# Layer 1's routed experts on gathered rows in plain f32, with the shared expert behind the last head

## The reference

```python
aff = jax.nn.sigmoid(flat_x @ gate_w + expert_bias)
_, topk_idx = jax.lax.top_k(aff, TOP_K)                    # TOP_K = 2
mask = (topk_idx[:, :, None] == jnp.arange(E_r)[None, None, :]).any(axis=1)
_, sel_idx = jax.lax.top_k(jnp.where(mask, aff, -1.0).T, capacity)   # 1024 // 7 = 146
kept = jnp.take_along_axis(mask.T, sel_idx, axis=1)
w = jnp.where(kept, jnp.take_along_axis(aff.T, sel_idx, axis=1), 0.0)
out = jax.vmap(_ffn)(flat_x[sel_idx], routed_w1, routed_w2)   # x1 * silu(x2) @ w2, F = 128
routed_sum = jnp.zeros_like(flat_x).at[sel_idx].add(out * w[:, :, None])
x = x + attention + (shared_sum + routed_sum)
```

## Time and profile before

| | |
|---|---|
| median of 3 runs | 812.11 us (811.54 to 812.62) |
| the profiled execution | 811.76 us, span 809.8 us |
| PE busy | 726.8 us, 4180 matmuls |
| DVE, ACT, POOL busy | 549.9, 370.9, 337.7 us |
| layer-1 experts, about | 557 to 637 us |

### The profile page before, as it was taken

One profiled execution on the slowest core, in us unless ns is written; L12 is line 12 of the kernel. 1 busy time (PEld: TensorE's weight loads), 2 busy tenths in 40 slices (PEclk: granted clock), 3 DMA queues, 4 the chain that ended last, 5 costly groups with the idle time before them and its releaser, 6 DMA issues.

```text
span 809.8 us, 12520 instructions
## 1 busy us (share of the span) xinstructions
PE 726.8 (90%) x4180; PEld 572.4 (71%) x4180; DVE 549.9 (68%) x1099; ACT 370.9 (46%) x783; POOL 337.7 (42%) x250
## 2 busy tenths in 40 slices
PE   3899999999889999999999999998999899765467
PEld 1455666678568888888888999987889446554356
DVE  4256566540679889897979667673667744499995
ACT  2264111110356474747474747555554531576541
POOL 0000375600167565656566666552111110337661
PEclk9999999999899999999999999999999999978798
DMA  9400000000310101010101000001110000100001
GB/s 311 186 1 2 1 1 1 1 1 1 103 46 21 33 19 32 19 32 19 32 19 32 20 32 19 19 7 40 40 39 0 1 0 1 33 1 0 0 1 52
DMA packets 11327, 24.75 MB, mean 31 GB/s; under 512 B 1217, under 2 KB 5538, under 8 KB 10786
## 3 DMA queue, kind: packets, MB, share of 16 engines
q1 hardware_dynamic: 10928, 23.19, 8.7%
q10 hardware_dynamic: 370, 1.18, 0.5%
HBM read 23.31 MB, written 1.05 MB: 30 GB/s over the span
## 4 chain that ended last, share of the span: by engine, by line
PE 66%; DVE 21%; issue 7%; ACT 3%; DMA 2%; POOL 1%; DVEq 1%; SPq 0%; POOLq 0%; ACTq 0%
PE bank L474 11%; PE bank L493 8%; PE bank L495 8%; PE bank L494 8%; PE bank L483 7%; PE bank L661 4%; PE bank L570 3%; PE bank L691 2%; PE bank L690 2%; DVE x L1439 2%; PE bank L675 2%; DVE zone L1616 2%; PE bank L537 2%; DVE arena L1423 1%; DVE arena L1413 1%
## 5 line engine op out<-in xcount | busy, mean ns | idle before, releaser
L493 PE MATMUL bank<-zone 128*128 128x256 f32 (+1 forms) x520 | 180.5, 347 | 9.5 <-DVE arena L1414 4.3
L495 PE MATMUL bank<-zone 128*128 128x256 f32 (+1 forms) x520 | 170.0, 327 | 0.0
L494 PE MATMUL bank<-zone 128*128 128x256 f32 (+1 forms) x520 | 169.8, 327 | 0.0
L493 PEld LDWEIGHTS bank<-zone 128*128 128x128 f32 x520 | 99.5, 191 | 26.1 <-DVE arena L1414 9.8
L1750 POOL TENSOR_TENSOR arena<-arena 128x512 f32<-128x512 f32 x64 | 82.0, 1282 | 84.3 <-ACT arena L1048 75.5
L495 PEld LDWEIGHTS bank<-zone 128*128 128x128 f32 x520 | 99.5, 191 | 8.8
L494 PEld LDWEIGHTS bank<-zone 128*128 128x128 f32 x520 | 99.7, 192 | 6.6
L1755 POOL TENSOR_TENSOR arena<-arena 128x512 f32<-128x512 f32 x64 | 82.4, 1287 | 32.3 <-DVE arena L1414 23.1
L1744 POOL TENSOR_TENSOR zone<-arena,zone 128x512 fp32r<-128x512 f32 (+1 forms) x56 | 58.4, 1056 | 60.8 <-ACT zone L1110 47.9
L474 PE MATMUL bank<-xT,arena 128*128 128x512 f32 x160 | 78.1, 626 | 1.5 <-ACT xT L937 0.8
L1067 ACT ACTIVATE arena<-arena 128x256 f32<-128x256 f32 (+1 forms) x128 | 62.1, 487 | 32.8 <-DVE arena L1423 32.7
(11 more groups left out here) (266 smaller groups left out, 1460.6 us busy)
## 6 DMA issues: line engine op xcount, KB each, us to landing
arena<-in_qk SPq DMA_DIRECT2D x16, 256.0 KB, 2.7
arena<-in_tern SPq DMA_DIRECT2D x1, 3072.0 KB, 21.9
arena<-in_wv SPq DMA_DIRECT2D x8, 256.0 KB, 2.7
arena<-in_wo SPq DMA_DIRECT2D x16, 128.0 KB, 2.1
arena<-in_w SPq DMA_DIRECT2D x8, 256.0 KB, 2.8
lB<-in_lB SPq DMA_DIRECT2D x1, 1288.5 KB, 24.3
arena<-in_lA SPq DMA_DIRECT2D x1, 1282.5 KB, 15.2
x<-in_x SPq DMA_DIRECT2D x1, 1024.0 KB, 12.8
```

Source lines behind the costliest of these rows:

```text
L493: pe.matmul(dst, lhi, rhi, start=(n == 0), stop=False)
L494: pe.matmul(dst, lhi, rlo, start=False, stop=False)
L495: last = pe.matmul(dst, llo, rhi, start=False, stop=(n == len(terms) - 1 and not open_end))
```

## The change

- The choice: `weigh_tokens` also scans, per expert, the number of each chosen token and adds 146 times the expert (C_OFF), which gives each (token, expert) a slot of 1022, or 0.
- Routes: after head 10 PE turns weights and slots (`turn_routes`, 16 transposes), waits for DVE's copies (`wcol_ready`), and DVE makes from them for each token two row indices (`idx`) and two weights (`wtok`) (`find_rows`).
- Scatters: POOL sends the normalised rows, 16 indirect DMAs of 128 rows, into `xg_rows` in DRAM, in heads 11, 12 and 13. A token without a slot is skipped by the bounds check. SP loads the rows back, by slot, as `xg`.
- Between heads 13 and 14: PE transposes `xg`, and runs the seven routed experts on 146 columns each, in plain f32. Each result is stored by SP in `y_rows`, as 80 and 66 rows. Row 1022 is zero.
- POOL then gathers for each token its two rows (16 indirect DMAs), before, between and behind the turnings of head 14; DVE adds them by weight: the first ones in head 15, the second ones before the shared expert's result is added.
- The shared expert, still split, comes after head 15. The Fori loops of the heads stop earlier, and heads 10 to 15 are partly straight code. The head's queue orders are otherwise as before.
- SP's loads: all routed weights at once, 3584 columns at the start of the layer and 1792 behind the gathered rows, in place of a pair of experts at a time.
- The arenas move: xT now also holds `xg`, and xn1 the second gather; qraw has room of its own.

```diff
+        xg_rows = nc.dram_tensor("xg_rows", (T, D), F32, kind="Internal").ap()
+        y_rows = nc.dram_tensor("y_rows", (SLOTS + 1, D), F32, kind="Internal").ap()
...
+            sp.wait_ge(kvbd_ready, 1)
+            sp.dma_start(xg_rows.rearrange("(t p) d -> p t d", p=P), kvbd[:, 0:1, :].to_broadcast([P, NT, D])).then_inc(rows_cleared, 16)
+            sp.dma_start(y_rows[SLOTS:SLOTS + 1, :], kvbd[0:1, 0, :]).then_inc(rows_cleared, 16)
...
+            sp.dma_start(wr[0], dram["wr"][:, 0:EXP_A]).then_inc(wr_loaded, 16)
+            with sp.Fori(0, SPLIT // 2) as i:
+                next_wv(i)
...
+                    next_wqk(i * 2 + c)
+                    next_wo(i * 2 + c)
+            next_wqk(SPLIT)
+            sp.wait_ge(scattered, 2 * NT * 16)
+            sp.dma_start(xg, xg_rows.rearrange("(t p) d -> p t d", p=P)).then_inc(xg_loaded, 16)
+            sp.dma_start(wr[1], dram["wr"][:, EXP_A:]).then_inc(wr_loaded, 16)
+            sp.wait_ge(wv_split, H1 // 2)
+            sp.dma_start(w1s, dram["w1s"]).then_inc(w1s_loaded, 16)
+            sp.wait_ge(wqk_split, H1)
+            sp.dma_start(w2s, dram["w2s"]).then_inc(w2s_loaded, 16)
+            for e in range(ER):
+                sp.wait_ge(*g_r2[e].ready)
+                sp.dma_start(y_rows[e * CAP:e * CAP + LEAD, :], yg[0:LEAD, e, 0:D]).then_inc(y_stored, 16)
+                sp.dma_start(y_rows[e * CAP + LEAD:(e + 1) * CAP, :], yg[2 * LEAD - CAP:LEAD, e, D:2 * D]).then_inc(y_stored, 16)
+            next_wo(SPLIT)
...
+            def turn_routes():
+                pe.wait_ge(wsel_ready, 1)
+                pe.wait_ge(rope_half, 4 * (ROUNDS // 2 + 2) + 3)
+                for n, table in enumerate((wT1, sT)):
+                    for t in range(NT):
+                        at = (n * NT + t) * ER
+                        last = pe.transpose(ps[0][:, at:at + ER], table[:, tok(t)], ident[0:ER, 0:ER])
+                last.then_inc(bank_full[0], 1)
+            def routed_in(e):
+                g = g_r1[e]
+                reuse(g)
+                for n in range(2):
+                    for k in range(KD):
+                        last = pe.matmul(g.ps[:, n * CAP:(n + 1) * CAP], expert(e, k * D + n * P, P), xgT[:, k, e * CAP:(e + 1) * CAP],
+                                         start=(k == 0), stop=(k == KD - 1))
+                last.then_inc(g.full_sem, 1)
+            def routed_out(e):
+                g = g_r2[e]
+                reuse(g)
+                pe.wait_ge(rhid_ready, e + 1)
+                for n, at in enumerate((0, CAP - LEAD)):
+                    last = pe.matmul(g.ps[0:LEAD, n * D:(n + 1) * D], rhid[e % 3][:, at:at + LEAD], expert(e, KD * D, D), start=True, stop=True)
+                last.then_inc(g.full_sem, 1)
...
+            with pe.Fori(0, SPLIT // 2 - 2) as i:
-            head(H1 // 2 - 1, 0)
-            head(H1 // 2 - 1, 1, False, False)
+            head(SPLIT // 2 - 2, 0)
+            turn_routes()
-            with pe.Fori(0, E1 // 2) as i:
+            head(SPLIT // 2 - 2, 1)
+            head(SPLIT // 2 - 1, 0)
+            head(SPLIT // 2 - 1, 1)
+            pe.wait_ge(xg_loaded, 16)
+            for b in range(NB):
+                for k in range(KD):
+                    g = g_tx[b][k]
+                    reuse(g)
+                    for tt in range(TPB):
+                        last = pe.transpose(g.ps[:, tok(tt)], xg[:, b * TPB + tt, tok(k)], ident)
+                    last.then_inc(g.full_sem, 1)
+            pe.wait_ge(wr_loaded, 16)
+            for e in range(ER):
+                if e == 0:
+                    pe.wait_ge(xg_act, KD)
+                if e == BW // CAP:
+                    pe.wait_ge(xg_dve, KD)
+                if e == EXP_A // EXP_W:
+                    pe.wait_ge(wr_loaded, 32)
+                routed_in(e)
+                if e >= 2:
+                    routed_out(e - 2)
+            routed_out(ER - 2)
+            routed_out(ER - 1)
+            for left in HEAD1["left"]:
+                pe.wait_ge(*left)
+            head(H1 // 2 - 1, 0, True, True, HEAD1)
+            head(H1 // 2 - 1, 1, False, False, HEAD1)
+            shared_in()
+            shared_out()
...
+            def routed_silu(e):
+                g = g_r1[e]
+                act.wait_ge(*g.full)
+                if e >= 3:
+                    act.wait_ge(*g_r2[e - 3].full)
+                act.activation(rhid[e % 3], g.ps[:, CAP:2 * CAP], ACT.Silu).then_inc(rsilu_ready, 1)
+            def keep_y(e):
+                g = g_r2[e]
+                act.wait_ge(*g.full)
+                act.activation(yg[0:LEAD, e, :], g.ps[0:LEAD, :], ACT.Copy).then_inc(g.ready_sem, 1)
+            for e in range(ER):
+                routed_silu(e)
+                if e >= 2 and e % 2 == 0:
+                    keep_y(e - 2)
+            keep_y(ER - 1)
+            act.wait_ge(w1s_loaded, 16)
+            act.activation(w1s2[0].bitcast(F32R), w1s, ACT.Copy).then_inc(w1s_hi, 1)
+            act.wait_ge(w2s_loaded, 16)
+            act.activation(w2s2[0].bitcast(F32R), w2s, ACT.Copy).then_inc(w2s_hi, 1)
...
+            dve.wait_ge(rows_cleared, 32)
...
+                chain(dve.scalar_tensor_tensor(out=wT1, in0=sT[:, 0:T], scalar=TAKEN, in1=sT0, op0=ALU.is_equal, op1=ALU.mult))
+                chain(dve.tensor_scalar(sT0, wT1, 0.0, None, ALU.is_gt))
+                chain(dve.tensor_tensor_scan(affT, sT0, sT0, 0.0, ALU.add, ALU.max))
+                dve.scalar_tensor_tensor(out=sT[:, 0:T], in0=affT, scalar=const[0:ER, C_OFF:C_OFF + 1], in1=sT0,
+                                         op0=ALU.add, op1=ALU.mult).then_inc(wsel_ready, 1)
+            def find_rows():
+                dve.wait_ge(bank_full[0], TURNED)
+                step(dve.tensor_copy(kwt, ps[0][:, 0:NT * ER].rearrange("p (t e) -> p t e", t=NT)), dve_done)
+                k = step(dve.tensor_copy(ktab, ps[0][:, NT * ER:2 * NT * ER].rearrange("p (t e) -> p t e", t=NT)), dve_done)
+                after(k)
+                dve.sem_inc(wcol_ready, 1)
+                chain(dve.tensor_reduce(dest[:, 0, :], ktab, AX.X, ALU.max))
+                chain(dve.tensor_reduce(dest[:, 1, :], ktab, AX.X, ALU.add))
+                chain(dve.tensor_tensor(dest[:, 1, :], dest[:, 1, :], dest[:, 0, :], ALU.subtract))
+                chain(dve.tensor_tensor(kown, ktab, dest[:, 0, :].unsqueeze(2).to_broadcast([P, NT, ER]), ALU.is_equal))
+                chain(dve.tensor_tensor(kown, kwt, kown, ALU.mult))
+                chain(dve.tensor_tensor(kwt, kwt, kown, ALU.subtract))
+                step(dve.tensor_reduce(wtok[:, 0, :], kown, AX.X, ALU.add), dve_done)
+                step(dve.tensor_reduce(wtok[:, 1, :], kwt, AX.X, ALU.add), dve_done)
+                chain(dve.tensor_scalar(miss, dest, 0.0, float(SLOTS + 1), ALU.is_equal, ALU.mult))
+                chain(dve.scalar_tensor_tensor(out=dest, in0=dest, scalar=-1.0, in1=miss, op0=ALU.add, op1=ALU.add))
+                dve.tensor_copy(idx.rearrange("p (s t) -> p s t", s=2), dest).then_inc(idx_ready, 1)
+            def add_rows(s, t):
+                dve.wait_ge(gathered[(s * NT + t) // TPB], TPB * 16)
+                dve.scalar_tensor_tensor(out=x[:, t, :], in0=got[s][:, t, :], scalar=wtok[:, s, t:t + 1], in1=x[:, t, :],
+                                         op0=ALU.mult, op1=ALU.add).then_inc(combined, 1)
...
+                if last:
+                    x_is(4 * h + base["added"])
+                    for t in range(NT):
+                        add_rows(0, t)
...
+            def routed_product(e):
+                g = g_r1[e]
+                dve.wait_ge(*g.full)
+                dve.wait_ge(rsilu_ready, e + 1)
+                dve.tensor_tensor(rhid[e % 3], g.ps[:, 0:CAP], rhid[e % 3], ALU.mult).then_inc(g.ready_sem, 1)
+            for e in range(ER):
+                routed_product(e)
...
+            x_is(4 * H1 + HEAD1["added"])
+            for t in range(NT):
+                add_rows(1, t)
+            for p in range(NT // 2):
+                dve.wait_ge(combined, NT + 2 * p + 2)
+                x_is(g_s2[p].ready[1] - 1)
+                add_pair(g_s2[p], p)
+                x_is(g_s2[p].ready[1])
+                measure((2 * p, 2 * p + 1))
+                if p % 2:
+                    normalise(2, xn2, p // 2)
...
+            def send_rows(ns):
+                for n in ns:
+                    pool.indirect_dma_start(xg_rows, bass.IndirectOffsetOnAxis(idx[:, n:n + 1], 0), xn1[:, n % NT, :], None,
+                                            bounds_check=SLOTS - 1, oob_is_err=False).then_inc(scattered, 16)
+            def fetch_rows(ns):
+                for n in ns:
+                    pool.indirect_dma_start(got[n // NT][:, n % NT, :], None, y_rows, bass.IndirectOffsetOnAxis(idx[:, n:n + 1], 0),
+                                            bounds_check=SLOTS, oob_is_err=False).then_inc(gathered[n // TPB], 16)
+            def beside_head(h, base=HEAD0, between=lambda: None):
```

(23 more changed lines are left out.)

342 lines of the change are left out of this document (170 added, 172 removed).

## The result

The changed kernel takes **791.29 us** (median of 4 runs, 790.22 to 795.84), the kernel before beside it on the same chip 811.92: a ratio of 0.9758, 95% interval 0.9732 to 0.9785. It is faster by 2.4%, 20.6 us. The forecast was 780 with 767 to 797: right in sign, 11 us too hopeful. The profiled execution of after took 792.32 against 811.76, a gain of 19.4; it is the one that I take apart.

A forecast was written before the change was run, and what follows sets the result against it. PE, busy 90% of 809.8 us, was taken to bound the kernel. The sum was 811.8 - 58.5 + 1 + 3 + 14 + 1.8 + 7.2 = 780.3, so 780 us, range 767 to 797.

The forecast's parts named there:

- Removed, 58.5: Last head's output product (end S) to layer 2's second transpose block: 25 us in place of 83.5, so 58.5 saved.
- (a), (b): Tables in head 9, 1 us reaching PE; turning the routes after head 10, 3 us with a lower clock.
- (c): Routed experts between heads 13 and 14: 14 us added, 6.6 for seven experts' products, 3 for clock and late load.
- (d): Row DMAs in POOL's queue ahead of weights PE wants: 1.8 us in head 12, 7.2 in heads 14 and 15.
- E: Time one row DMA holds POOL: taken as 1.1 us, with 0.33 and 2.6 kept as bounds.
- free up to E = 1.6: Head 11: five scatters on POOL cost PE nothing unless each holds POOL longer than 1.6 us.
- Rival 1: Gathers cheap, each holding POOL 0.65 us or less: heads 14 and 15 lose nothing, 772 or 768 us; chance 20%.
- rival 3: POOL held for each row DMA's whole transfer: stalls in heads 11 to 15, slower, 819 us at 2.6 each; chance 4%.
- my own case: Each row DMA holds POOL between 0.7 and 1.4 us: 773 to 789 us overall; chance 55%.
- rival 2: Queue dear, still a gain: each row DMA holds POOL 1.4 to 2.2 us, 790 at 1.6, 808 at 2.2; chance 20%.
- Rival 5: Gathered rows load in 10 us, not 5.5: PE stands 3 to 4 us before the routed transposes, 784; no separate chance.
- Rival 4: DVE and POOL block each other during head 15's row adds: at most 3 us more, 783; no separate chance.

The follow-up runs named there:

- Two cures, on two queues: Changed kernel with SP asking for the wqk load ahead of the output weights: 783.46 us; or POOL's two inner scatters moved behind the output-weight split: 785.02 us.
- one exchange of two lines: Changed kernel with SP asking for the next query and key weights ahead of the output weights: 783.46 us.
- 2.9 and 0.5 alone, 8.6 together: Changed kernel with second gathers behind head 15's output-weight split, 788.42 us; head 14's inner four behind its split, 790.76; both plus SP's load order, 774.90.

## Why the prediction was right or wrong

*Removed, 58.5.* Right. From the end of the last output product (597.4) to the second block it is 25.4 us, forecast 25: first product, wait of 2.17 for the split (2.2), first transposes at S+17 (614.35), all as worked out. Not worked out was that PE comes back from its wait of 4.00 ahead of these transposes at a clock of 0.57, for 2.2 us. Of the 2.0 us missing in the table, 1.5 are the output product itself, 5.6 us at a clock of 0.50 and not 4.1.

*(a), (b), tables and routes, 4.* 2.0. The wait behind the transposes is 0.66, as before, and the clock that I feared from the earlier trace rows stayed at 1.00 in head 11's first 20 us.

*(c), routed experts, 14.* 16.1, and the nearness is luck. "Per expert four plain-f32 products of 146 columns ... 0.125 and two of 256, 0.94" is wrong by half: it is 1.86, seven make 13.0. The step that failed is the reading of the earlier trace rows: "x4, 0.86" is two matmuls with two records each, so 0.43, not 0.215, and the 0.11 that I set beside it for 128 columns is a transpose's, not a matmul's. The count could have told me: L661 has 256 records, and the code asks for eight such products in each of 16 heads. The 3 us for a lower clock and a late load did not come (clock 1.00; the rows' load is asked for at 531.46 and takes 6.8), and covered the error.

I wrote that the trace contradicts the rule of the Trainium skill, "FP8 and Floating Point Precision" (TensorE Precision Notes), of 4 passes for true FP32. The trace bears it out: 0.43 against 0.12 is 3.6, 0.25 against 0.065 is 3.8, and the seven experts' 13.0 us are near the 14 that I worked out from it. What I called a contradiction was my count.

*(d), row DMAs.* The mechanism was right: POOL's own queue ahead of wo and wqk. The size was off. With E = 1.30 the formulas give 2.2 for head 12 (measured 2.1) and 16 x 1.3 - 10.4 = 10.4 for heads 14 and 15 (10.1), where 1.1 had given 1.8 and 7.2: 3 us of the miss. PE's waits for POOL in heads 12, 14 and 15 sum to 8.4 us, inside the 3 to 20 that I had set. The formula for heads 14 and 15 knew the last due time alone; head 14 has one of its own, which costs nothing more in the changed kernel but decides what a cure is worth. Head 13's wo split was in time, as said; that head lost 1.7 to the clock behind head 12's wait, which no term of mine had.

*Head 11, "free up to E = 1.6".* The step that failed, for 6.6 us: by its own rule head 11 should have lost nothing at 1.30. I had asked when PE wants POOL's results, and not who else waits for them: SP stands at the wo split with the wqk load behind it, ACT at the load with the values behind it. "SP's own queue waits only for what POOL has done by then" was the sentence, and nothing in it had been worked out. Two cures, on two queues, show it.

*Rivals.* Rival 1 (cheap gathers) and rival 3 (held for the whole transfer) are out: a pitch of 1.30, nearly the same for half the rows. E came within the 0.7 to 1.4 of my own case, but the time lies outside the 773 to 789 that I gave this case. It is about that of rival 2 (790 at E = 1.6), by another way, so it is partly luck that the full range, which rival 2 had stretched to 797, holds it. Rival 5 did not come: PE went from head 13 to the transposes without a wait. Rival 4 did not decide either; DVE's row adds show in PE's waits only once the gathers are out of the way.

**The sum again:** 811.8 + 2.0 + 6.6 + 2.1 + 2.1 + 16.1 + 10.1 - 56.5 - 1.8 = 792.5, with 792.32 in the profile. Of the 12 us between this and the forecast's 780.3, head 11 is 6.6, the size of E 3.2 (2.9 in heads 14 and 15, 0.3 in head 12), the clock behind waits about 3.2 (1.7 in head 13, 1.5 at the output product), the experts 2.1, and 0.9 has no term (0.4 more in head 13, 0.5 behind the output product); the tables and the routes give 2.0 back and the rest of layer 2 and 3 another 1.8.

## What to carry to other kernels

When work is put ahead of something on one queue, list everyone who waits for that something, the load queue included, and then what stands behind each waiter in its own order. A load should be asked for in the order in which its buffer comes free: here one exchange of two lines was worth 7.8 us, more than a third of what the whole change had gained.

Where an engine has several due times in a row, clearing one queue shows its worth only when the others are cleared too (2.9 and 0.5 alone, 8.6 together). And count a line's records against the matmuls that the code asks for before dividing a row's time by its count.
